# Attention in parts of 8, 4 and 4 tiles, most of the WKV recurrence spread over its second half, and P·V issued behind the V projection

## What is computed

```python
q, k = rope(rmsnorm(h @ wq.T)), rope(rmsnorm(h @ wk.T))      # h = layernorm(x); 16 heads of 128
s = 50 * tanh(q @ k.T * scale / 50); p = softmax(causal(s))
x = x + (p @ (h @ wv.T)) @ wo.T
# WKV over the 128 tokens of a tile, k = layernorm(x), v = ctx, per channel:
no = max(o, u + k); A = exp(o - no); E = exp(u + k - no)
y = (A*p + E*v) / (A*q + E)
no2 = max(w + o, k); p, q, o = exp(w+o-no2)*p + exp(k-no2)*v, exp(w+o-no2)*q + exp(k-no2), no2
x = x + y
# h = layernorm(x); 16 experts of width 352, 6 for each token, and a shared one of width 704
x = x + sum_e combine[:, e] * (silu(h@w1g[e].T) * (h@w1u[e].T)) @ w2[e].T + shared(h)
```

## Time and profile before

| | |
|---|---|
| median of 3 runs | 2392.84 us (2389.02 to 2394.59) |
| the profiled execution: its time, its span | 2396.61 us, 2394.8 us |
| attention steps, 48.0 to 1020.6 us | 972.6 us |
| recurrence, 1020.6 to 1355.1 us | 334.5 us |
| routing, scatters, rest of the shared expert, to 1619.1 us | 264.0 us |
| sparse part, to the end | 775.7 us |

### The profile page before, as it was taken

How to read it: one execution, slowest core, us unless ns; L and a number is a source line. 1 busy time by engine, 2 the same in 40 slices (tenths; PEclk the granted TensorE clock), 3 DMA queues, 4 the chain that set the end, 5 groups by cost and what they waited for, 6 DMA issues and landing times. The chain is left out here.

```text
span 2394.8 us, 43437 instructions
## 1 busy us (share of the span) xinstructions
PE 2060.7 (86%) x12188; PEld 1849.8 (77%) x12189; DVE 1191.2 (50%) x2389; ACT 892.2 (37%) x2127; POOL 997.2 (42%) x1124
## 2 busy tenths in 40 slices
PE   3999999999999999933665830599999999999998
PEld 3888888888888888823555730599999999998887
DVE  5555555555555555579999610443333333333322
ACT  4555445554454445524334100123333333333322
POOL 3333333333333333335455177004334243268874
PEclk9999999999999999955767865799999999999999
DMA  8544444444444444401212255234434344478897
GB/s 308 175 155 155 157 160 160 160 160 156 155 155 155 160 160 160 149 6 52 97 49 97 80 218 225 80 117 129 134 117 147 121 129 129 127 175 202 194 208 198
DMA packets 182577, 351.45 MB, mean 147 GB/s; under 512 B 19456, under 2 KB 72960, under 8 KB 182528
## 3 DMA queue, kind: packets, MB, share of 16 engines
q1 hardware_dynamic: 129056, 240.60, 30.2%
q0 software_dynamic: 21504, 51.13, 9.1%
q10 hardware_dynamic: 31968, 59.12, 7.6%
HBM read 206.60 MB, written 144.18 MB: 146 GB/s over the span
## 5 line engine op out<-in xcount | busy, mean ns | idle before, releaser
L1211 PE MATMUL bank<-w_hi,xT 128*128 x1776 | 476.5, 330 | 14.4 <-issue 12.8
L411 PE MATMUL bank<-w_hi,xT 128*128 128x512 f32 x1024 | 349.5, 402 | 6.0 <-DMA xT<-xT_att 6.0
L674 DVE TENSOR_TENSOR hT<-bank,hT 128x384 fp32r<-128x384 f32 x143 | 79.6, 556 | 539.7 <-ACT hT L671 467.7
L1211 PEld LDWEIGHTS bank<-w_hi,xT 128*128 128x128 f32 x1776 | 316.5, 189 | 34.3 <-issue 32.0
L584 POOL TENSOR_TENSOR rr<-rr,expo 128x4 f32<-128x4 f32 x128 | 128.9, 1007 | 392.2 <-DVE rr L524 392.2
L1211 PE MATMUL bank<-w_lo,xT 128*128 x888 | 287.1, 323 | 0.0
L1221 PE MATMUL bank<-w_hi,hT 128*128 x666 | 228.6, 397 | 2.1 <-DVE hT L674 2.1
L411 PEld LDWEIGHTS bank<-w_hi,xT 128*128 128x128 f32 x1024 | 193.7, 189 | 47.0 <-issue 6.4
L671 ACT ACTIVATE hT<-bank 128x384 fp32r<-128x384 f32 x143 | 70.2, 491 | 392.0 <-PE bank L664 306.9
L453 PE MATMUL bank<-w_hi,xT 128*128 128x256 f32 x1024 | 209.3, 287 | 0.0
L411 PE MATMUL bank<-w_lo,xT 128*128 128x512 f32 x512 | 202.3, 395 | 0.0
(11 more groups left out here) (210 smaller groups left out, 4711.9 us busy)
## 6 DMA issues: line engine op xcount, KB each, us to landing
xT<-xT_att SPq DMA_DIRECT2D x128, 512.0 KB, 3.5
xg<-aA SPq DMA_DIRECT2D x128, 264.0 KB, 3.5
yg<-aA SPq DMA_DIRECT2D x128, 256.0 KB, 3.7
xnB<-xg ACTq DMA_DIRECT2D x111, 264.0 KB
raw<-in_weights SPq DMA_DIRECT2D x176, 136.0 KB
xT<-xT_ffn SPq DMA_DIRECT2D x32, 512.0 KB
yg<-a ACTq DMA_DIRECT2D x56, 256.0 KB
yg<-e ACTq DMA_DIRECT2D x55, 256.0 KB
```

The source lines that it names most:

```text
L411: last = pe.matmul(bank[par][:, :], xT[:, par, a, c * P:(c + 1) * P], w_hl[w][:, fw, c * 512:(c + 1) * 512], start=n == 0, stop=n == 11)
L674: dve.tensor_tensor(hT[:, 1, :], src[:, 0:IP], hT[:, 0, :].bitcast(F32), ALU.subtract).then_inc(hT_lo, 1)
L1211: last = pe.matmul(out_[:, 0:I], xT[:, par, a, c * P:(c + 1) * P], flat(w_hl[w])[:, bass.ds(at + (c * 2 * I + half_ * I), I)], start=n == ...
```

## The change

- The weights of a head group come in 8 pieces of 544 columns (`HB`, `PIECE`). Steps 0 to 63 do all 8 groups for tiles 0 to 7, one piece for each step. Steps 64 to 127 (`SPLIT`) do them for tiles 8 to 11 and again for 12 to 15, four steps for each group, so two pieces for each step (`pieces_of`, `place_of`); the weights are loaded and split three times in place of once. The zero stores are made in the first half, twice the size.
- P·V is issued behind the V projection, ahead of `wo`. `wo` and the transposes of q and k share a bank (`QY_`), with new waits.
- The recurrence is cut into slots, pairs 11 apart (`PITCH`): scans and products of a pair stand in its own 11, the division's end, the way back to rows, the residual, norm and gate in the next ones. One slot stands in each step from 64 on (`rec_pe`, `rec_act`, `rec_pool`, `rec_dve`, `rec_sp`), the rest, two to a step, in the first 20 steps of the shared expert, whose 32 steps now all follow attention.
- The reciprocal of the denominator is exp(-ln d) on ACT with one Newton step on ACT, DVE and POOL. The difference k - o moved from DVE's L911 to POOL, its clamps with the bias `u` to ACT.
- Normed rows of the first five pairs go to DRAM (`xn_rows`) and come back behind attention. At most four scatters are under way at a time (`scattered[n % 4]`).
- The matmuls of the sparse part, its blocks and its gathers are the same.

```diff
+HB = B // 2
...
-PIECE = WCOLS // B
+PIECE = WCOLS // HB
...
+        SPLIT = NSTEP_B // 2
+        PITCH = 11
...
+        def pieces_of(s):
+            if not isinstance(s, int) or s < SPLIT:
+                return [s + HB]
+            i = s - SPLIT
+            return [SPLIT + HB + 2 * i - 2, SPLIT + HB + 2 * i - 1] if i else []
+        def place_of(s):
+            if s < SPLIT:
+                return (s // HB) % 2, s % HB, (s // HB) % NG
+            i = s - SPLIT
+            return (i // 4) % 2, HB + 4 * (i // 32) + i % 4, (i // 4) % NG
...
+        def rec_pe(pe, w, at):
+            p, r = w // PITCH, w % PITCH
+            q, k = p, p - 1
+            front, back, far = p < NQ, 0 <= k < NQ, 0 <= k - 1 < NQ
+            if at == "end" and r == 0 and front:
+                pe.wait_ge(ln_done, 2 * call_front(q) + 1)
+                if far:
+                    pe.wait_ge(loW, 2 * k)
+                wait(pe, res_done, 2 * q - 2)
+                transposes(pe, R_, lambda c: lnf(0)[:, c, :], trK)
+            if at == "mid" and r == 1 and front:
+                pe.wait_ge(ln_done, 2 * call_front(q) + 2)
+                pe.wait_ge(kT_in, 2 * q + 1)
+                transposes(pe, R_, lambda c: lnf(1)[:, c, :], trK)
...
+        def rec_act(act, w, at):
+            p, r = w // PITCH, w % PITCH
+            q, k = p, p - 1
...
+            if r in (5, 6):
+                c = 2 * (r - 5) + (at == "second")
+                seg_c = slice(2 * c, 2 * c + 2)
+                if c == 0:
+                    act.wait_ge(d_done, q + 1)
+                    if q:
+                        act.wait_ge(pm_done, q)
+                    else:
+                        act.wait_ge(xg_zero, 16 * NSTEP_B)
+                act.activation(aA[:, seg_c, :], dE[:, seg_c, :], ACT.Relu, bias=ucol[:, c:c + 1]).then_inc(amin, 1)
+                act.wait_ge(amin, KC * q + c + 1)
+                act.activation(dE[:, seg_c, :], dE[:, seg_c, :], ACT.Relu, scale=-1.0,
+                               bias=nucol[:, c:c + 1]).then_inc(emin, 1)
+            if at == "first" and r == 7:
+                act.activation(aA[:, :, :], aA[:, :, :], ACT.Exp, scale=-1.0).then_inc(aA_done, 1)
+            if at == "second" and r == 7:
+                act.wait_ge(emin, KC * q + KC)
+                act.activation(dE[:, :, :], dE[:, :, :], ACT.Exp, scale=-1.0).then_inc(dE_done, 1)
+            if at == "second" and r == 8:
+                act.wait_ge(den_done, q + 1)
+                act.wait_ge(e2v_done, q + 1)
+                act.activation(e2[:, :, 1:T + 1], qS[:, :, 0:T], ACT.Ln).then_inc(ln_den, 1)
+            if at == "first" and r == 9:
+                act.wait_ge(ln_den, q + 1)
+                act.activation(e2[:, :, 1:T + 1], e2[:, :, 1:T + 1], ACT.Exp, scale=-1.0).then_inc(inv_done, 1)
+            if at == "second" and r == 9:
+                act.wait_ge(rec_done, q + 1)
+                act.activation(qS[:, :, 0:T], qS[:, :, 0:T], ACT.Copy, scale=-1.0, bias=2.0).then_inc(two_done, 1)
...
+        def rec_pool(pool, w):
+            p, r = w // PITCH, w % PITCH
+            q, k = p, p - 1
+            if r == 0 and 0 <= k < NQ:
+                pool.wait_ge(num_done, k + 1)
+                pool.wait_ge(inv_done, k + 1)
+                pool.tensor_tensor(pS[:, :, 0:T], pS[:, :, 0:T], e2[:, :, 1:T + 1], ALU.mult).then_inc(first_done, 1)
...
+            if r == 2:
+                pool.wait_ge(o_scan, q + 1)
+                pool.tensor_tensor(a2[:, :, 1:T + 1], oS[:, :, 0:T], oS[:, :, 1:T + 1],
+                                   ALU.subtract).then_inc(d2_done, 1)
+            if r == 3:
+                pool.tensor_tensor(e2[:, :, 1:T + 1], kS[:, :, 1:T + 1], oS[:, :, 1:T + 1],
+                                   ALU.subtract).then_inc(e2a_done, 1)
+            if r == 4:
+                pool.tensor_tensor(dE[:, :, :], kS[:, :, 1:T + 1], oS[:, :, 0:T], ALU.subtract).then_inc(d_done, 1)
...
+                pool.tensor_tensor(vS[:, :, :], dE[:, :, :], vS[:, :, :], ALU.mult).then_inc(ev_done, 1)
+            if r == 9:
+                pool.wait_ge(ev_done, q + 1)
+                pool.wait_ge(pm_done, q + 1)
+                pool.tensor_tensor(pS[:, :, 0:T], pS[:, :, 0:T], vS[:, :, :], ALU.add).then_inc(num_done, 1)
...
+        def rec_dve(dve, w):
...
+            if r == 9:
+                dve.wait_ge(inv_done, q + 1)
+                dve.tensor_tensor(qS[:, :, 0:T], qS[:, :, 0:T], e2[:, :, 1:T + 1], ALU.mult).then_inc(rec_done, 1)
...
-                        dve.reciprocal(qS[:, :, 0:T], qS[:, :, 0:T]).then_inc(rec_done, 1)
...
+        def rec_slots(t):
+            return [SPLIT + 2 * t, SPLIT + 2 * t + 1] if t < ROUTE_AT else [None] * 2
...
+                def step(s, par, fw, b, g):
+                    front, mid, back, tail, rec = wants(s)
+                    if front:
+                        if isinstance(s, int) and s >= SPLIT and (s - SPLIT) % 4 == 0:
+                            need = SPLIT + HB if s == SPLIT else SPLIT + HB + 2 * (s - SPLIT - 1)
+                        else:
+                            need = s + HB if b == 0 else None
+                        if need is not None:
+                            pe.wait_ge(piece_hi, need)
+                            pe.wait_ge(piece_lo, need)
...
+                    if mid:
+                        pe.wait_ge(k_out, s)
+                        pe.wait_ge(rot_done, 2 * s)
+                        wait(pe, acc_done, s - 3)
+                        transposes(pe, QY_, lambda c: rot[:, c * P:(c + 1) * P], t_done)
+                    if front:
+                        wait(pe, v_hi, s)
+                        wait(pe, v_lo, s)
...
+                        last.then_inc(v_done, 1)
+                    if back:
+                        pe.wait_ge(p_hi, s - 1)
+                        pe.wait_ge(p_lo, s - 1)
+                        pe.wait_ge(v_hi, s - 1)
+                        pe.wait_ge(v_lo, s - 1)
...
+                        last.then_inc(pv_done, 1)
+                    if rec:
+                        rec_pe(pe, s - SPLIT, "mid")
+                    if tail:
+                        pe.wait_ge(oT_hi, s - 2)
+                        pe.wait_ge(oT_lo, s - 2)
+                        if mid:
+                            pe.wait_ge(qkT_hi, s)
+                            pe.wait_ge(qkT_lo, s)
...
+                    if front:
+                        act.wait_ge(qk_done, s + 1)
+                        wait(act, ss_done, s)
+                        act.activation(sq, bank[par][:, :], ACT.Square).then_inc(sq_done, 1)
...
+                        for n in pieces_of(s):
+                            if isinstance(n, int):
+                                piece_act(act, n - n % 2, n % 2, (n // HB) % 2, bass.ds(n % HB * PIECE, PIECE))
+                            else:
+                                piece_act(act, n - par, par, 1 - fw, bass.ds(b * PIECE, PIECE))
+                    if rec:
+                        rec_act(act, s - SPLIT, "first")
+                    if front:
...
-                act.wait_ge(scattered, 16 * TOPK * B)
+                for i in range(4):
+                    act.wait_ge(scattered[i], 16 * TOPK * B // 4)
...
+                def step(s, par, fw, b, g):
+                    front, mid, back, tail, rec = wants(s)
+                    if front:
+                        pool.wait_ge(ms_done, s + 1)
+                        pool.tensor_tensor(rr[:, :], rr[:, :], expo[:, :], ALU.pow).then_inc(pw_done, 1)
+                        wait(pool, th_done, 2 * s - 2)
+                        pool.wait_ge(pw_done, s + 1)
+                        pool.tensor_tensor(rk[:, par, :], rr[:, HG:4], kscale[:, :], ALU.mult).then_inc(rms_done, 1)
+                        for i, n in enumerate(pieces_of(s)):
+                            if i == 1:
+                                continue
+                            if isinstance(n, int):
+                                piece_pool(pool, n, n % 2, (n // HB) % 2, bass.ds(n % HB * PIECE, PIECE))
+                            else:
+                                piece_pool(pool, n, par, 1 - fw, bass.ds(b * PIECE, PIECE))
+                    if mid:
+                        pool.wait_ge(ex_done, s)
+                        pool.tensor_tensor(heads(ex), heads(ex), mask[:, :, :], ALU.mult).then_inc(mask_done, 1)
+                    if front and len(pieces_of(s)) > 1:
+                        n = pieces_of(s)[1]
+                        piece_pool(pool, n, n % 2, (n // HB) % 2, bass.ds(n % HB * PIECE, PIECE))
+                    if rec:
+                        rec_pool(pool, s - SPLIT)
...
+                        wait(pool, scattered[n % 4], 16 * (n // 4))
```

More of the change, by code:

```diff
@@ L1259, in step, with hook, shared_step @@
+                attention(act, step)
+                def hook(slot):
+                    if slot is not None:
+                        rec_act(act, slot, "first")
```

(18 more changed lines are left out.)

1132 lines of the change are left out of this document (530 added, 602 removed).

## The result

The changed kernel takes 2451.62 us (median, 2445.12 to 2457.87), the kernel before 2392.79: ratio 1.0248, 95% interval 1.021 to 1.0285. It is 2.5% slower; 2312 us was forecast. The profiled execution took 2446.02 us, span 2444.2.

A forecast was written before the change was run, and what follows sets the result against it. The prediction took TensorE to bound the kernel, except where the recurrence on DVE does. From a span of 2394.8 us, +3 +180 -155.5 -108 and 0 for the sparse part gave 2314.3, forecast as 2312 us; range 2205 to 2410.

The forecast's parts named there:

- (d): Routing, scatters and shared steps, 264.0 us: the scatters would bound it at 156 us, so -108 us.
- (c): Recurrence stretch, 334.5 us, goes; attention's last three steps and 20 shared steps with slots replace it: -155.5 us.
- (a): Attention steps 0 to 63: larger weight pieces on POOL delay the starts of 8 head groups slightly: +3 us.
- (b): Attention steps 64 to 127: repeated weight splits and a recurrence slot in each step lengthen them: +180 us.
- b2: Head-group starts in attention's second half: PE waits 3.44 us for POOL's second piece, then a lower clock: +74 us.
- b3: Attention's second half: the ring of two raw weight buffers delays loads, 0.7 us in each of 49 steps: +34 us.
- b6: Attention's second half: POOL and DVE slow each other, +0.17 us in each of 64 steps: +11 us.
- b4: Slot 8, second half: ACT's Ln waits for DVE ahead of the copy P·V needs, 4 us in 6 steps: +24 us.
- b5: Slot 1, second half: PE's second transposes wait for ACT's copy behind two weight pieces, 1.5 us x 6: +9 us.
- b7: The rest of attention's second half: more loads, doubled stores and P·V's new place, put at 0.
- C: Rival: TensorE stays at 1.2 GHz in attention's second half, 3.6 us more per step, 2542 with all 64; chance 0.15.
- D: Rival: the recurrence doesn't hide in shared steps; twelve take 12 us each, +40 us, 2352 us; chance 0.12.

The follow-up runs named there:

- e2_xfirst: Changed kernel with the tile's load issued ahead of the two weight loads in shared steps: ratio 1.0307 to the kernel before.
- a0_after: The changed kernel, unaltered, run again beside the kernel before on the experiments' chips: 2378.81 us, ratio 1.04.
- b0_before: The kernel before, unaltered, traced on the experiments' chips: 2286.48 us.
- a1_after: The changed kernel, unaltered, run once more: 2400.14 us in its one execution, ratio 1.0485 to the kernel before.
- e1_need: Changed kernel; a head group's first q and k projection in the second half waits only for its own pieces: 2326.79 us, ratio 1.0166.
- e10_smallpieces: e6_three with ACT and POOL splitting only 8 of 544 columns of each weight piece in attention's second half: ratio 0.9751 to the kernel before.
- e4_notable: Changed kernel with Ln and the Exp behind it replaced by copies, so no table loads: ratio 1.0366 to the kernel before.
- e7_lnlate: e6_three with ACT's Ln of slot 8 moved behind the copy of P: ratio 0.9977 to the kernel before.
- e8_pvold: e6_three with P·V back ahead of the V projection: ratio 1.004 to the kernel before.
- e6_three: Changed kernel with e1_need's and e2_xfirst's edits, three slots per shared step and routing seven steps earlier: 2272.68 us, ratio 0.9935.
- e9_nolimit: e6_three without the limit of four scatters under way: ratio 0.9936 to the kernel before.

## Why the prediction was wrong

**The step that failed is (d)**, "the third stretch, 264.0 us": 264.0 - 156 = -108. The 156 us were right (without the long waits 132.9 + 2.3 us from the first scatter, behind some 25). The 264.0 were not the program's. 107 us of them came from waits that "no engine's instruction ended": I saw the row and took the stretch as it stood, then let the waits vanish with the shared steps. On the chips of the experiments the kernel before needs about 160 us there (1353 to 1512.7), and the change wins next to nothing. In the first measurement the waits stayed: 79.3 us behind the last scatter where 9.9 were forecast, with four shared steps in them. "At up to 110 they still fit beside the scatters" is false there and true in the later runs. By either reckoning the sum loses its largest gain but one; without it the forecast would have been 2420, slower than the kernel before by 1.1%.

**(c) was too small by 49 us**: the 20 shared steps and what follows took 255.4 us to the first scatter instead of 206.7. The prediction looked at PE's inserts and the recurrence's chain and not at SP's queue: two weight loads that wait for the splits stand ahead of the tile's load. 36 of the 49 lie in the first four shared steps (70.4 us, 34.8 forecast), 9 in the other sixteen. e2_xfirst gives back 18 to 26 of the 49 by the first scatter. The rest was not taken apart.

**(a)** was small, as forecast: 3 us forecast, 6.8 more in a0_after than in b0_before. **(b)**, +180, came out as a sum: 185.5 measured for steps 64 to 127 (188.3 in a0_after, 198.7 in a1_after). That is in part luck, for the terms stand otherwise. PE was busy for 478.6 us of this window before and for 560.3 of 664.1 after. The 28 us of inserts come off by count; the other 54 are, by estimate, the lower clock, where the forecast had 22 (15 x 1.5). The last 104 are PE's idle time.

- b2, 74: the mechanism is shown, and its size is 61 by e1_need. The wait was longer than forecast (4.67 us for 3.44 in the place above).
- b3 and b6, 45 together: e10_smallpieces takes away all that the splits do and gives 39, so the two are shown in sum only. ACT stood 63.6 us in 43 places of a0_after's second half for the raw loads, which is b3's ring. b6 was far too small as a delay of the chain: beside the other engine's work POOL's mask and DVE's low part of P took (b0_before, then a0_after)

```profile
L592 POOL TENSOR_TENSOR pS<-pS,mask 128x256 f32<-128x256 f32 x63 | 46.6, 739 | 107.3 <-ACT pS L502 107.3
L556 DVE TENSOR_TENSOR pT<-pS,pT 128x256 fp32r<-128x256 f32 x63 | 26.8, 425 | 128.8 <-ACT pT L505 128.8
...
L1321 POOL TENSOR_TENSOR ex<-ex,mask 128x256 f32<-128x256 f32 x63 | 76.9, 1221 | 110.4 <-ACT ex L1219 110.4
L1450 DVE TENSOR_TENSOR pT<-ex,pT 128x256 fp32r<-128x256 f32 x63 | 77.3, 1228 | 58.2 <-ACT pT L1225 58.2
```

Together that is 1.3 us a step in mean by which P comes later, where b6 had 0.17. That the two engines slow each other is read from their overlap (POOL was at work for over half the length of 62 of these 63 low parts); no run separates it.

- b4, 24: the mechanism held, in the step of slot 9: P·V waited 11.6 us there in a0_after. The table loads had no part in it (e4_notable), and what it costs in all is not shown, since moving Ln behind the copy cost more (e7_lnlate).
- b5, 9: PE waited 3.8 us for ACT's copy in the steps of slot 1, and 7.3 in those of slot 0, which had no term.
- b7, 0: P·V's new place is worth 22 us (e8_pvold); in its old place (b) would have been over 200.

With e1_need and e2_xfirst in it, the window of e6_three is still 129 us longer than before (607.8 - 478.6). 28 are PE's inserts by count and 39 the splits'; 62 remain for the slots' waits and the clock of 0.96, and these weren't tried apart.

**Rivals.** C: PEclk was 0.92 in the second half. 1.2 GHz came for stretches like the 5.3 us above, not for whole steps, and the 54 us that it cost are well short of C's break-even, 22 steps of 3.6 us; C gave the right sign, and a part of the cause. B fell (e9_nolimit). A fell. D was nearest to the truth of (c), but the pace was set by SP's queue in part; with that mended and three slots a step the 13 steps of e6_three still took 11.7 us each (from 1182.0 to 1333.8), more than PE's work.

**Open:** what ends the long waits beside the scatters. They were there in the first measurement for both kernels and in no later run. That they belong to the occasion is shown; whether to that chip or to something else, and whether the scatters or anything of the program make them possible, is not.

## What to carry to other kernels

A wait that no instruction of the program ends is not the program's to win: take it out of the stretch before counting what a change gives back, and give the outcome in which it stays a chance of its own. When a wait is written as "all pieces", ask which columns the next matmuls read: two waits in place of one gave back 2.3%. When work is moved into a loop, write down what each queue issues in a step, in order, with what it waits for; a load behind a waiting load is late by the whole wait.
